# A four-layer graph network on one core: the turned x read from memory, the digraph row inverses on VectorE, the minus adjacency on ScalarE, and a new order

## What is computed

```
u = einsum('bid,bjd->bij', h, h) / temper
delta = softmax(u) * adjacency_matrix
attn = delta / (sum(delta, axis=-1) + 1e-10)
ctx = (attn * upper) @ hl + diag(attn) * hs + (attn * lower) @ hr
h = relu(layernorm(ctx) * g + beta)
```

## Time and profile before

| | |
|---|---|
| median of 3 executions | 2644.26 us (2640.42 to 2648.33) |
| the profiled execution | 2648.33 us, of which its span is 2646.3 us |
| PE busy | 2513.5 us, 95% of the span |
| POOL busy | 2230.9 us, 84% |
| DVE busy | 2112.3 us, 80% |
| ACT busy | 2075.7 us, 78% |
| DMA queue of SP | 50.3% of the 16 DMA engines' time |

### The profile page before, as it was taken

One profiled execution on the slowest core, in us unless ns is written; L12 is line 12 of the kernel. 1 busy time (PEld: TensorE's weight loads), 2 busy tenths in 40 slices (PEclk: granted clock), 3 DMA queues, 4 the chain that ended last, 5 costly groups with the idle time before them and its releaser, 6 DMA issues.

```text
span 2646.3 us, 91774 instructions
## 1 busy us (share of the span) xinstructions
PE 2513.5 (95%) x33856; PEld 1892.1 (71%) x33856; DVE 2112.3 (80%) x8230; ACT 2075.7 (78%) x5844; POOL 2230.9 (84%) x3340
## 2 busy tenths in 40 slices
PE   5799999999999999999999999999999999999985
PEld 4667677777777777777777777777777777777753
DVE  6687787877778888888888888888888888888874
ACT  6667877778778888888888788788788888888765
POOL 5488888888888898898888888888888888888874
PEclk9899999999999999999999999999999999999997
DMA  6834545545445555545545555554545555554533
GB/s 176 176 68 83 97 85 97 96 83 97 89 87 97 95 90 97 97 89 95 97 89 100 93 90 98 96 91 93 96 95 92 93 99 88 96 97 88 94 55 71
DMA packets 846822, 251.63 MB, mean 95 GB/s; under 512 B 805552, under 2 KB 845616, under 8 KB 846384
## 3 DMA queue, kind: packets, MB, share of 16 engines
q1 hardware_dynamic: 837920, 230.83, 50.3%
q10 hardware_dynamic: 8464, 14.94, 1.9%
HBM read 35.92 MB, written 12.58 MB: 18 GB/s over the span
## 4 chain that ended last, share of the span: by engine, by line
POOL 35%; PE 23%; DVE 16%; ACT 13%; issue 7%; DMA 5%; SPq 1%; DVEq 0%; ACTq 0%; POOLq 0%
POOL region L750 6%; ACT region L870 5%; DMA region<-region 4%; POOL region L739 4%; DVE region L1138 4%; PE bank L966 3%; PE bank L957 3%; PE bank L968 3%; PE bank L967 3%; PE bank L959 3%; PE bank L958 3%; ACT region L876 3%; POOL ab L766 3%; POOL region L790 2%; DVE small L1144 2%
## 5 line engine op out<-in xcount | busy, mean ns | idle before, releaser
L957 PE MATMUL bank<-region,w_hi 128*128 128x128 f16 x3960 | 690.4, 220 | 35.6 <-DVE w_lo L1075 14.0
L959 PE MATMUL bank<-region,w_lo 128*128 128x128 f16 x3960 | 690.0, 220 | 0.0
L958 PE MATMUL bank<-region,w_hi 128*128 128x128 f16 x3960 | 690.0, 220 | 0.0
L966 PE MATMUL bank<-w_hi,region 128*128 128x384 f16 x1815 | 595.5, 328 | 10.4 <-DMA region<-region 9.2
L967 PE MATMUL bank<-w_lo,region 128*128 128x384 f16 x1815 | 594.3, 327 | 0.0
L968 PE MATMUL bank<-w_hi,region 128*128 128x384 f16 x1815 | 594.2, 327 | 0.0
L750 POOL TENSOR_TENSOR region<-region 128x512 f16<-128x512 f32 x330 | 382.9, 1161 | 117.7 <-ACT region L876 116.6
L870 ACT ACTIVATE region<-region,small 128x128 f32<-128x128 f32 x1320 | 419.2, 389 | 53.6 <-DVE small L1144 44.1
L957 PEld LDWEIGHTS bank<-region,w_hi 128*128 128x128 f16 x3960 | 389.4, 98 | 60.8 <-issue 36.2
L958 PEld LDWEIGHTS bank<-region,w_hi 128*128 128x128 f16 x3960 | 389.8, 98 | 14.8 <-issue 9.9
L959 PEld LDWEIGHTS bank<-region,w_lo 128*128 128x128 f16 x3960 | 389.9, 98 | 0.0
(11 more groups left out here) (246 smaller groups left out, 8238.0 us busy)
## 6 DMA issues: line engine op xcount, KB each, us to landing
region<-region SPq DMA_TRANSPOSE x825, 3.0
last_unit<-w_dram ACTq DMA_DIRECT2D x19, 576.0 KB, 6.2
x<-x_dram SPq DMA_DIRECT2D x55, 192.0 KB, 2.3
out_dram<-region SPq DMA_DIRECT2D x55, 192.0 KB, 2.2
adj<-adj_dram SPq DMA_DIRECT2D x55, 64.0 KB, 2.2
mask<-adj_t_dram SPq DMA_DIRECT2D x55, 64.0 KB, 2.4
rows<-rows_dram ACTq DMA_DIRECT2D x5, 576.0 KB, 4.4
last_unit<-last_unit SPq DMA_TRANSPOSE x135, 3.1
```

Source lines behind the costliest of these rows:

```text
L957: pe.matmul(dst, lhsT=w_hi[:, w, k, cols], rhs=t_hi[u][:, k, :], start=(k == 0), stop=False)
L958: pe.matmul(dst, lhsT=w_hi[:, w, k, cols], rhs=t_lo[u][:, k, :], start=False, stop=False)
L959: last = pe.matmul(dst, lhsT=w_lo[:, w, k, cols], rhs=t_hi[u][:, k, :], start=False, stop=(k == DT - 1))
L966: pe.matmul(dst, lhsT=t_hi[u][:, k, :], rhs=w_hi[:, w, k, :], start=(k == 0), stop=False)
```

## The change

- **Turn 0.** The host hands over a second copy of the input, with each item already turned (`x_t_dram`, 128 rows of 1536 contiguous bytes). A new step `load_turned` reads it into the item's `z` tile; ACT casts from there straight into `t_hi`, POOL subtracts into `t_lo`, and PE waits for the POOL step. The transpose of turn 0 is gone. `load_turned` waits for `norm` 3 of the item seven before, the last reader of `z`. `load` (x and adj) now waits for the cast of turn 0 of its own item, and `bias_x` 0 waits for `load`.
- **Row inverses.** `sums` on POOL is gone. `delta_di` on DVE gets two more instructions on 128 x 1 columns behind its own: a scalar_tensor_tensor (ZSUM and DSUM, both in `small`) and a reciprocal, each after a wait for the one before.
- **Minus adjacency** moves from POOL (tensor_scalar) to ACT (Copy with scale -1).
- **Order.** All due times in `PARTS` and `SHIFTED` are new, and PERIOD is 22.0511 in place of 22.1046. The first use of a weight now waits for its true place in the order.

The core of the diff:

```
-    (SYNC, "load", 0): (-309.759, 0.900, 3.290, (), ((VECTOR, "residual", 3),)),
+    (SYNC, "load", 0): (-52.181, 0.900, 3.000, ((SCALAR, "turn", 0),), ()),
+    (SYNC, "load_turned", 0): (840.461, 0.450, 2.900, (), ((SCALAR, "norm", 3),)),
-    (PE, "project", 0): (-137.817, 1.513, 1.710, ((SYNC, "turn", 0),), ()),
+    (PE, "project", 0): (-158.359, 1.513, 1.710, ((POOL, "turn", 0),), ()),
-    (PE, "project", 2): (-135.670, 1.466, 1.660, ((SYNC, "turn", 0),), ()),
+    (PE, "project", 2): (-377.663, 1.466, 1.660, ((POOL, "turn", 0),), ()),
-    (VECTOR, "delta_di", 0): (147.540, 0.206, 0.503, ((SCALAR, "u_di", 0),), ()),
-    (POOL, "sums", 0): (-457.777, 0.870, 0.950, ((VECTOR, "delta_di", 0),), ()),
+    (VECTOR, "delta_di", 0): (-205.622, 0.500, 0.580, ((SCALAR, "u_di", 0),), ()),
-    (POOL, "minus_adj", 0): (55.594, 0.515, 0.770, ((VECTOR, "delta_gcn", 1),), ()),
+    (SCALAR, "minus_adj", 0): (574.038, 0.190, 0.300, ((VECTOR, "delta_gcn", 1),), ()),
...
-            def load(i, k):
+            def load_turned(i, k):
                 if i == UNITS - 1:
                     sp.wait_ge(w_lo_made, NW)
                 if i >= UNITS:
-                    sp.wait_ge(*mixed_out.at(i - UNITS, "added", 3))
+                    sp.wait_ge(*scalar_done.at(i - UNITS, "normed", 3))
+                sp.dma_start(x_t[i % UNITS], x_t_d[i]).then_inc(loaded.of(i), 16)
+
+            def load(i, k):
+                sp.wait_ge(*cast.at(i, "x", 0))
                 sp.dma_start(x[i % UNITS], x_d[i]).then_inc(loaded.of(i), 16)
                 sp.dma_start(adj[i % UNITS], adj_d[i]).then_inc(loaded.of(i), 16)
...
                 pool.wait_ge(*cast.at(i, "x", k))
+                if k == 0:
+                    pool.tensor_tensor(t_lo[u], x_t[u], t_hi[u], ALU.subtract).then_inc(low_made.of(i), 1)
+                    return
...
+                if k == 0:
+                    pool.wait_ge(*loaded.at(i, "in"))
                 pool.tensor_tensor(x[u], x[u], rows[:, X_BIAS[k], :], ALU.add).then_inc(low_made.of(i), 1)
...
-            def minus_adjacency(i, k):
-                u = i % UNITS
-                pool.wait_ge(*mixed_out.at(i, "delta_gcn", 1))
-                pool.tensor_scalar(minus_adj[u], adj[u], -1.0, None, ALU.mult).then_inc(gpsimd_done.of(i), 1)
-
-            def denominator(i, layer):
-                u = i % UNITS
-                pool.wait_ge(*mixed_out.at(i, "delta_di", layer))
-                pool.tensor_scalar(col(u, DENOM), col(u, ZSUM), 1e-10, col(u, DSUM), ALU.mult, ALU.add).then_inc(gpsimd_done.of(i), 1)
-                pool.wait_ge(*gpsimd_done.at(i, "sum", layer))
-                pool.tensor_tensor(col(u, INVERSE), col(u, DENOM), constant(MINUS_ONE), ALU.pow).then_inc(gpsimd_done.of(i), 1)
...
                 if k == 0:
-                    act.wait_ge(*loaded.at(i, "in"))
-                    src = x
+                    act.wait_ge(*loaded.at(i, "turned"))
+                    act.activation(t_hi[i % UNITS], x_t[i % UNITS], ACT.Copy).then_inc(cast.of(i), 1)
+                    return
...
+            def minus_adjacency(i, k):
+                u = i % UNITS
+                act.wait_ge(*mixed_out.at(i, "delta_gcn", 1))
+                act.activation(minus_adj[u], adj[u], ACT.Copy, scale=-1.0).then_inc(scalar_done.of(i), 1)
...
             def project(i, w):
                 if (w, i) == first(PE, "project", w):
-                    pe.wait_ge(w_lo_made, PLACE[w] + 1)
-                pe.wait_ge(*landed.at(i, "x", TURN_OF[w]))
+                    pe.wait_ge(w_lo_made, nth(VECTOR, w))
+                if TURN_OF[w] == 0:
+                    pe.wait_ge(*low_made.at(i, "x", 0))
+                else:
+                    pe.wait_ge(*landed.at(i, "x", TURN_OF[w]))
...
                 dve.tensor_tensor_reduce(out=delta_of(i, layer), in0=e_of(i, "u_di", layer), in1=adj[u], scale=1.0, scalar=0.0, op0=ALU.mult,
-                                         op1=ALU.add, accum_out=col(u, DSUM)).then_inc(mixed_out.of(i), 1)
+                                         op1=ALU.add, accum_out=col(u, DSUM)).then_inc(numbers.of(i), 1)
+                dve.wait_ge(*numbers.at(i, "row sum", layer))
+                dve.scalar_tensor_tensor(col(u, DENOM), col(u, ZSUM), 1e-10, col(u, DSUM), ALU.mult, ALU.add).then_inc(numbers.of(i), 1)
+                dve.wait_ge(*numbers.at(i, "denominator", layer))
+                dve.reciprocal(col(u, INVERSE), col(u, DENOM)).then_inc(mixed_out.of(i), 1)
```

More of the change, by code:

```diff
@@ L97 @@
 PARTS = {
[L98 to L109, removed]
@@ new lines @@
+    (VECTOR, "divide", 0): (-193.800, 0.703, 1.005, ((SCALAR, "attend", 0), (SCALAR, "attend", 1), (SCALAR, "attend", 2)), ()),
+    (VECTOR, "residual", 1): (-193.415, 0.480, 0.620, ((VECTOR, "gain", 1),), ()),
+    (PE, "attend", 1): (-189.242, 0.330, 0.520, ((SYNC, "scores", 1),), ()),
+    (VECTOR, "add_bias", 11): (-185.685, 0.460, 0.560, ((PE, "project", 11), (POOL, "low", 9)), ()),
+    (POOL, "residual", 0): (-185.483, 1.050, 1.150, ((SCALAR, "spread", 0),), ()),
+    (VECTOR, "scores", 2): (-181.977, 0.850, 0.420, ((PE, "scores", 2), (POOL, "scores", 1)), ()),
@@ new lines @@
+    (POOL, "inner", 1): (-153.541, 0.520, 0.620, ((VECTOR, "inner", 1),), ()),
+    (SYNC, "turn", 6): (-153.275, 1.240, 3.600, ((POOL, "turn", 6),), ()),
+    (PE, "project", 4): (-151.555, 1.513, 1.710, ((SYNC, "turn", 1),), ()),
+    (SCALAR, "project", 2): (-147.807, 0.370, 0.570, ((PE, "project", 2),), ()),
+    (SYNC, "scores", 3): (-147.581, 1.240, 4.000, ((POOL, "scores", 3),), ()),
+    (SCALAR, "norm", 1): (-147.099, 0.599, 0.740, ((POOL, "residual", 1),), ()),
+    (POOL, "low", 0): (-146.800, 0.880, 1.130, ((SCALAR, "project", 0),), ()),
@@ new lines @@
+    (VECTOR, "project", 15): (-88.319, 0.463, 0.741, ((SCALAR, "project", 15),), ()),
+    (SCALAR, "attend", 4): (-88.253, 0.165, 0.450, ((PE, "attend", 4),), ()),
+    (VECTOR, "gain", 3): (-87.666, 0.525, 0.810, ((POOL, "inner", 3), (VECTOR, "centre", 3)), ()),
+    (SCALAR, "project", 12): (-86.546, 0.420, 0.530, ((VECTOR, "add_bias", 12),), ()),
+    (SCALAR, "norm", 3): (-85.685, 0.597, 0.740, ((POOL, "residual", 3),), ()),
+    (POOL, "turn", 3): (-84.784, 0.870, 1.112, ((SCALAR, "turn", 3),), ()),
@@ new lines @@
+    (SCALAR, "project", 17): (-83.750, 0.420, 0.620, ((VECTOR, "add_bias", 17),), ()),
+    (POOL, "low", 17): (-82.508, 0.880, 1.130, ((SCALAR, "project", 17),), ()),
+    (PE, "scores", 3): (-81.983, 0.360, 0.610, ((VECTOR, "project", 15), (VECTOR, "project", 16), (POOL, "low", 17)), ()),
+    (VECTOR, "delta_di", 1): (-81.385, 0.500, 0.580, ((SCALAR, "u_di", 1),), ()),
+    (PE, "u_di", 1): (-80.623, 0.512, 0.720, ((SYNC, "turn", 4),), ()),
+    (VECTOR, "inner", 0): (-80.295, 1.339, 1.705, ((PE, "mix", 0),), ()),
@@ new lines @@
+    (PE, "project", 16): (-77.729, 1.513, 1.710, ((SYNC, "turn", 5),), ()),
+    (SCALAR, "attend", 2): (-77.478, 0.165, 0.450, ((PE, "attend", 2),), ()),
+    (POOL, "low", 9): (-77.374, 0.880, 1.120, ((SCALAR, "project", 9),), ()),
+    (VECTOR, "delta_gcn", 1): (-77.370, 0.199, 0.407, ((SCALAR, "u_gcn", 1),), ()),
+    (POOL, "scores", 3): (-77.020, 1.150, 1.420, ((SCALAR, "scores", 3),), ()),
+    (VECTOR, "add_bias", 1): (-76.028, 0.460, 0.720, ((PE, "project", 1),), ((SYNC, "store", 0),)),
@@ new lines @@
+    (POOL, "residual", 1): (-74.064, 1.050, 1.150, ((SCALAR, "spread", 1),), ()),
+    (SCALAR, "turn", 4): (-73.449, 0.412, 0.600, ((VECTOR, "gain", 2),), ()),
+    (SCALAR, "attend", 1): (-71.523, 0.165, 0.450, ((PE, "attend", 1),), ()),
+    (SCALAR, "scores", 2): (-68.397, 1.920, 2.100, ((VECTOR, "scores", 2), (SYNC, "scores", 1)), ()),
+    (VECTOR, "add_bias", 17): (-67.461, 0.460, 0.720, ((PE, "project", 17),), ()),
+    (SCALAR, "project", 15): (-65.261, 0.371, 0.570, ((PE, "project", 15),), ()),
@@ new lines @@
+    (POOL, "low", 11): (18.582, 0.880, 1.120, ((SCALAR, "project", 11),), ()),
+    (PE, "project", 12): (20.703, 1.466, 1.660, ((SYNC, "turn", 4),), ()),
+    (VECTOR, "project", 6): (25.529, 0.466, 0.745, ((SCALAR, "project", 6),), ()),
+    (SCALAR, "spread", 0): (29.289, 0.830, 0.950, ((VECTOR, "residual", 0),), ()),
+    (POOL, "turn_delta", 0): (50.012, 1.120, 1.360, ((SYNC, "delta", 0),), ()),
+    (VECTOR, "centre", 3): (50.859, 0.525, 0.670, ((SCALAR, "inner_spread", 3),), ()),
+    (SCALAR, "attend", 5): (57.566, 0.165, 0.450, ((PE, "attend", 5),), ()),
@@ new lines @@
+    (SCALAR, "project", 7): (192.348, 0.371, 0.570, ((PE, "project", 7),), ()),
+    (SCALAR, "spread", 3): (197.945, 0.830, 0.950, ((VECTOR, "residual", 3),), ()),
+    (SCALAR, "delta", 1): (214.697, 0.190, 0.310, ((VECTOR, "delta_di", 1),), ()),
+    (POOL, "low", 12): (223.133, 0.880, 1.120, ((SCALAR, "project", 12),), ()),
+    (SCALAR, "norm", 2): (224.225, 0.598, 0.740, ((POOL, "residual", 2),), ()),
+    (SCALAR, "inner_spread", 2): (229.152, 0.800, 0.920, ((VECTOR, "inner", 2),), ()),
```

369 lines of the change are left out of this document (166 added, 203 removed), and 60 rows, old and new, of the table SHIFTED.

## The result

The changed kernel takes 3105.9 us (3101.09 to 3106.45 in 4 runs) where the kernel before took 2642.88 beside it: 1.1745 times as long, with an interval of 1.1722 to 1.1767. The prediction was 2630. All that follows is set against the earlier trace rows and its neighbours.

What follows compares the result with a forecast made beforehand. PE was taken as the bound, with 132.8 us idle to win. Terms -1 - 4 - 4 - 4 - 1 = -14 took 2648.3 to 2634.3 us; runs' median lies 4.1 below, hence 2630, range 2607 to 2658.

Steps and rivals of the forecast that it cites:

- the balance of relief, delay and new order there: From 132 to 2514 us: POOL's relief, DVE's added time and new order together give -4 us, ends -20 and +25.
- The start: First stretch: V's weight comes first, so PE starts at about 9.2 us instead of 14.0; -4 us, ends 0 and -5.
- The hole behind it: PE's `attend` waits after the start, up to 8.4 us for a late transpose, shrink: -4 us, ends -12 and +4.
- The sum: Whole kernel: the terms -1, -4, -4, -4 and -1 add to -14 us.
- The turned x in the long run: Turn 0 outside the start: transposes leave SP's queue, but the load may go later; about even, -1 us.
- The end: Last 132 us, items running alone: a shorter chain gives about -1 us, ends -8 and +6.
- SP held by the later load: Rival, SP's queue: waiting for `norm` 3 adds 2.9 us each, 28 us in all, total 2658 us; chance 0.06.
- VectorE held by GpSimd: Rival, new `delta_di` instruction: 0.25 us of wait reaches PE at 128 places, 32 us, total 2662 us; chance 0.11.
- Minus adjacency: 64 instructions moved to ACT at 0.33 us each, 0.3 us per item, hidden: zero, at most 1 us.
- POOL's relief: Middle: POOL loses 2.2 us of 34.3 per item, from 88% to 82% busy, worth something to PE.

Runs made afterwards that it cites:

- k4: Kernel before with old operations, laid out with only PE's due times set to the changed kernel's; 3102.4 us, ratio 1.1727.
- k9: Kernel before with one number changed, the due time of PE's `project` 1 (K) from -157.7 to +4.6; 2955.4 us, ratio 1.1156.
- k11: The ladder: kernel before with PE's due times in 38 equal steps from -157.7 to 13.5 in order of computation; 3116.7 us, ratio 1.1772.
- k10: Control: kernel before with one due time changed, PE's `attend` 4 from -6.9 to -376.1; 2651.1 us, ratio 1.0015.
- k14: As k12 with the same order, but the denominator is a tensor_scalar with one column as tensor input; 2627.6 us, ratio 0.9928.
- k15: As k14, but with an order fitted to the end time of the undisturbed plan alone; 2643.7 us, ratio 0.9979.
- k12: All three changed operations, with an order fitted to them by search from the old plan's beginnings; 2646.8 us, ratio 0.9998 to the kernel before.
- k13: Operations of the kernel before, with an order fitted by the same search as k12; 2625.2 us, ratio 0.9919 to the kernel before.
- k7: Kernel before with only the row inverses moved to VectorE, old lists kept except GpSimd's sums; 2652.9 us, ratio 1.0030.
- k16: As k7, but the denominator is a tensor_scalar with one column as tensor input; 2650.2 us, ratio 1.0005 to the kernel before.
- k8: Kernel before with only minus adjacency moved to ScalarE, old lists otherwise kept; 2647.2 us, ratio 1.0004.
- k5: All three changed operations, with an imitated order (due times are when the old plan began each step); 2721.9 us, ratio 1.0282 to the kernel before.
- k6: Kernel before with only x turned in memory, order imitated as in k5; 2704.4 us, ratio 1.0215.

## Why the prediction was wrong

**The step that failed** is the new order. The prediction had it inside one term, "-4 for the balance of relief, delay and new order there, with -20 and +25 as ends", and the ends came from waits in the trace of before. PE's due times alone are worth +17.3% (k4), some 457 us. The trace of before could not show that, but the listing could. The prediction read the new due times of V, Q and K (-377.7, -158.4 and 4.6) and used them only for the order of the weights at the start; it compared none of the new due times with those of the other items in work. K's number alone, in the old table, costs 11.6% (k9). The planner whose costs and due times stand in the kernel is itself a replay. Its own end, worked out from the listing, is 2616 us for before and 3090 for the changed kernel; for k4 3092 (measured 3102), for k9 2935 (2955), for k11 3108 (3117), for k10 2620 (2651).

**The start.** The first matmul came at 8.3 us (forecast 9 to 10), but PE idle of the first stretch is 45.6 us, not about 37: the new order has PE do nearly all of V, Q and K of the first six items first, so that the first `scores` came at 36.2 us where it came at 21.9 before, and the head start fed no attention chain. The hole behind it, put at -4, did not close: PE's waits of `attend` for turned probabilities are 20.1 us in place of 12.6. In k14 the idle time is 132.00 - 96.02 = 36.0. But k15, with the same operations and its first matmul at 8.4 us, has 45.6. So the earlier first matmul is shown, and whether its 8 us stay hangs on the order; the prediction took them as given by the operations.

**The sum** was -14 us, nearly all of it for the operations. With both orders fitted, the operations as the changed kernel has them are 21.7 us slower than the old ones (k12 against k13), and 2.4 slower without the GpSimd wait (2627.6 against 2625.2), which can't be told from nothing. No run shows the -14.

**The turned x in the long run** was put at -1. This was not isolated with a fitted order. The 8 us that k14 has over k13 in the start (36.0 us idle against 132.00 - 88.07 = 43.9) are taken back in the middle: from 132 to 2514 us PE is idle 48.2 us in k14 and 19.5 + 18.6 = 38.1 in k13.

**The end** was put at -1. PE's idle time in the last 132 us went from 39.0 to 63.4 us, outside the +6 that was left for it; in k13 and k14 it is 37.1 and 35.3.

**SP held by the later load** did not happen in the changed kernel. SP's waits there:

```profile
SPq L713 <- ACT region L886: 77.6, 31, 8.2
SPq L683 <- ACT region L841: 75.8, 33, 5.6
...
SPq L713 <- ACT last_unit L886: 22.7, 5, 9.2
```

`norm` 3 (L886) was waited for only by the store, 77.6 + 22.7 = 100.3 us in all, no more than the 102.6 for `residual` 3 before; `load_turned` stood behind it and waited for nothing. `load` (L683) waited 75.8 us for its cast, and 17.1 more in the seventh unit. What that costs by itself no run isolates.

**VectorE held by GpSimd** was a rival at 0.25 us of PE per place, 32 us. The mechanism is shown (k12 against k14, and less clearly k7 against k16), its size is 19.2 / 128 = 0.15 us per place in one order and 0.25%, some 7 us in all, in the other. The median of 0.46 us in k12 is over the 0.3 that was to show it; in the changed kernel, whose POOL is busy 70% of the middle and not 82% as in k12, it is 0.16. The page SBUF — State Buffer of the Trainium skill, section Who interferes with whom, lets a VectorE instruction with at most one SBUF input, outside the modes that use both ports, go free of GpSimd; k14 agrees, 212 to 215 ns in each of 110 places.

**Minus adjacency and POOL's relief** were right in size (k8: 1.0004; POOL at 1409.58 / 1720 = 82% in k14), and the relief gave PE nothing that shows.

**Open.** How the new due times starve PE is known only in part: the changed kernel bunches, and the ladder loses as much without bunches. Which of PE's new due times do the harm together was not run. With the imitated order the planner has 18 of the 75 us that k5 loses and 26 of the 57 of k6; the rest is not explained. Whether turned x, alone and fitted, would gain or lose was not tried.

## What to carry to other kernels

Where a kernel runs several items at once in a static order, a changed table of priorities is not a small unknown beside the operations: replay the order with the costs in the listing before pricing anything else. Looking at single priorities isn't enough; the ladder looked sensible and lost 17.7%. An operation can be judged only with orders fitted alike for both versions: with an imitated order the same three operations read +2.8%, with both orders fitted +0.8%, and +0.1% with the one-column denominator, while two fits of the same operations lie 0.5% apart. Keep a small two-column instruction on VectorE to one tensor input while GpSimd is busy.

## What the runs showed of the hardware

- A tensor_scalar on 128 x 1 columns with a per-row number took 212 to 215 ns beside a busy GpSimd, the scalar_tensor_tensor for the same arithmetic 158 ns at least and up to 1171 ns, with a median of 460 (k14, k12). The form that is 54 ns longer at its least made the kernel 19.2 us shorter in the same order.
- TensorE's granted clock followed the swings: 0.60 over the 20 us behind a stretch in which PE was busy for 14.3 of 20 us, and 1.00 again in the next. Over the middle the changed kernel had 0.93 in place of 1.00, and with it 142 us more of PE's busy time for the same matmuls.
- The planner, which in its play lowers TensorE's clock after idle time but knows nothing of GpSimd's hold, was within 1% for orders with a large loss (k4, k9, k11) and up to 88 us short where the loss is small (k5: 2634 planned, 2721.9 measured). It warned of the large loss and could not rank the last percent: k15 against k14.
